# The sort of a graph network's edges: key comparison and rank in six slices among the look-up steps

## The chip, the core and the metric

The kernel runs on one core of a Trainium2 chip. A core has five engines with queues of their own, which work beside one another and meet at semaphores: TensorE (PE, matrix products; its weight loads are listed as PEld), VectorE (DVE), ScalarE (ACT), GpSimd (POOL, here the issuer of indirect DMAs) and SyncE (SP, which issues plain DMAs). The metric is the device time of one execution in microseconds (us), the median of several runs; less is better.

## The reference

Four residual layers of a graph network over 12500 nodes and 412500 edges. Every layer normalises the node features, gathers over the edges and adds the result to `x`:

```python
h = jnp.maximum(_layernorm(x, axis=-1), 0.0)
x = x + _L0_gnn_ref(h, edge_weight1, src, dst, L0_gnn_W, L0_gnn_b)      # weighted sum by dst
h = jnp.maximum(_layernorm(x, axis=-1), 0.0)
x = x + _L1_gnn_ref(h, edge_index, edge_attr_32, L1_gnn_u, batch0, ...) # sum, max, mean of edge_attr by src
h = jnp.maximum(_layernorm(x, axis=-1), 0.0)
x = x + _L2_gnn_ref(h, L2_gnn_weight_r, src, dst, edge_type_8)          # one matrix per edge type
h = jnp.maximum(_layernorm(x, axis=-1), 0.0)
x = x + _L3_gnn_ref(h, L3_gnn_attn_l, L3_gnn_attn_r, src, dst)          # attention over dst
```

The edges come sorted by `dst`, so sums by `dst` are running sums. The second layer sums and maximises by `src`:

```python
seg_sum = jax.ops.segment_sum(edge_attr, row, num_segments=N)   # row = src
seg_max = jax.ops.segment_max(edge_attr, row, num_segments=N)
cnt = jax.ops.segment_sum(jnp.ones((edge_attr.shape[0], 1), ...), row, num_segments=N)
```

For it the kernel first puts the edge features in order of `src`. That sort is what the change touches.

## The kernel before

The padded edges lie on 128 partitions (P) of J columns each. All stages walk over the J columns in NCH = 54 chunks of L = 60 columns; a chunk is 128 x 60 = 7680 edges. Stages follow one another with a barrier between:

- the first third of the weighted sum (`gathered_layer("wsum", ...)`, 18 chunks), in which PE also counts how many edges each source has (matmuls at L706), while POOL gathers rows with 60 indirect DMAs per chunk (L403);
- the sort, `scatter_by_source` (L717 to L940), from about 1850 to 7060 us;
- the other two thirds of the weighted sum, now with the scans over the sorted rows beside it; then the layers with types and with attention.

**What the sort does.** For every edge it works out its place in the array `by_src` and POOL scatters the edge's 33 numbers there. The place is: start of the source's run, plus the edges of this source in earlier columns, plus those in the same column on earlier partitions. The last part is the rank in the column.

Earlier columns: a running count per source lies in the PSUM tile `pC`, laid out as 128 rows (source number modulo 128) by 98 (source number over 128), in WAYS = 4 streams side by side, since columns are taken four at a time. A chunk has STEPS = 15 steps of four columns. For one step, ACT copies the counts (`sort_cnt`, L892, `snapshot`); PE adds the step's edges with four matmuls of one-hots (`low`, `high` into `pC`, L926, `update`) and looks the counts up with matmuls of `lowT` against the copy (into one of three tiles `pG`, L934, `look_up`; each is shown as two in the trace, so eight per step); DVE multiplies by the one-hot `high` (`sort_prod`, L843, `weigh`) and sums it (`sort_place`, L850, `pick`). I count the steps from zero. PE may run three look-ups ahead of `weigh`; the next snapshot waits for the update before it.

The rank in the column: SP loads for each partition the source numbers of all partitions before it (`sort_keys`, 7680 int16 each, 1920 KB) and DVE compares them with the partition's own (L834), then sums over the 128 (L836, into `sort_rank`). The tile is compared in place. The transposed one-hot `lowT` comes from another load, the low seven bits of all edges of the chunk (`sort_lows`, 960 KB, L828).

**Order on DVE**, for every chunk: split the source numbers (L815 to L819), `low` (L824), `high` (L825), `lowT` (L828), comparison (L834), rank (L836), then the 15 steps, each a `weigh` followed by the `pick` of the step before, and at the end `hand_on` (L857), which adds place and rank into `sort_place_i`.

**Order on the others.** SP (L773 to L777) waits until the rank of the chunk before is made, loads keys and low bits under one semaphore, then the features (`sort_feat`, 960 KB). POOL waits for `sort_place_i` and issues 60 scatters (L787), 128 rows each; the places and rows have two buffers, and `hand_on` needs POOL to be a quarter into the batch before. So DVE and PE work on chunk k+1 while POOL scatters chunk k. ACT fills the rows to be scattered from the features in between (L900).

Of the kernel before, what the change touches and what calls it, by code (L numbers as in the profile page):

```python
# [14 lines left out]
P = 128  # L15
# [28 lines left out]
def build(nc, x, src, dst, etype, weight, attr, W0, b0, u, W1, b1, W2, b2, Wr, attn_l, attn_r, out, L):  # L44
# [31 lines left out]
    with ctx:  # L76
# [640 lines left out]
        def scatter_by_source(lead_chunk):  # L717
# [7 lines left out]
            with ExitStack() as c:  # L725
# [3 lines left out]
                def sem(name):  # L729
# [23 lines left out]
                pC = ps("pC", [P, 512], F32, c)  # L753
                loaded = [sem(f"loaded{s}") for s in range(2)]
                scattered = [semaphore(f"scattered{s}") for s in range(2)]
                (rows_ready, rows_used, split, parted, keys_loaded, matched, ranked, ones_ready, based, snapped, updated, summed,
                 picked, placed, place_ready, issuing) = (
                    sem(n) for n in ("rows_ready", "rows_used", "split", "parted", "keys_loaded", "matched", "ranked", "ones_ready",
                                     "based", "snapped", "updated", "summed", "picked", "placed", "place_ready", "issuing"))
                block = phase(c)  # L760
                PIECES = 4
                PIECE = L // PIECES
                earlier_keys = bass.AP(tensor=key_rows.tensor, offset=0, ap=[[L, P], [2 * P * L, NCH], [1, P * L]])
                every_low = bass.AP(tensor=low_rows.tensor, offset=0, ap=[[0, P], [P * L, NCH], [1, P * L]])

                @block.sync
                def _(sp):
                    with sp.Fori(0, NCH // 2) as i:
                        for s in range(2):
                            k = 2 * i + s  # L770

                            sp.wait_ge(ranked, k + 1)
                            sp.dma_start(keys[:].unsqueeze(1), earlier_keys[:, bass.ds(k, 1), :]).then_inc(keys_loaded, 16)  # L773
                            sp.dma_start(lows[:].unsqueeze(1), every_low[:, bass.ds(k, 1), :]).then_inc(keys_loaded, 16)

                            sp.wait_ge(rows_ready, k + 1)
                            sp.dma_start(feat[s][:], attr.rearrange("(p j) f -> p j f", p=P)[:, bass.ds(k * L, L), :]).then_inc(loaded[s], 16)  # L777
# [31 lines left out]
                def _(dve):  # L809
                    v = nc.vector  # L810

                    def one_hots(k):

                        dve.wait_ge(ranked, k + 1)
                        v.tensor_scalar(parts_i[:, 0, :], src_all[:, bass.ds(k * L, L)], 127, None, ALU.bitwise_and)  # L815
                        v.tensor_scalar(parts_i[:, 1, :], src_all[:, bass.ds(k * L, L)], 7, None, ALU.logical_shift_right)
                        v.tensor_copy(parts[:, 2, :], src_all[:, bass.ds(k * L, L)]).then_inc(split, 1)
                        dve.wait_ge(split, k + 1)
                        v.tensor_copy(parts[:, 0:2, :], parts_i[:]).then_inc(parted, 1)  # L819
                        dve.wait_ge(parted, k + 1)  # L820
                        dve.wait_ge(updated, STEPS * k + 1)
                        part = lambda m, w: parts[:, m, :].unsqueeze(2).to_broadcast([P, L, w])
                        iota = lambda w: iota_b[:, 0:w].unsqueeze(1).to_broadcast([P, L, w])
                        v.tensor_tensor(low[:], iota(P), part(0, P), ALU.is_equal)  # L824
                        v.tensor_tensor(high[:], iota(HT), part(1, HT), ALU.is_equal)  # L825

                        dve.wait_ge(keys_loaded, 32 * k + 32)
                        v.tensor_tensor(lowT[:], lows[:].rearrange("p (x j) -> p j x", j=L),  # L828
                                        own_near.unsqueeze(2).to_broadcast([P, L, P]), ALU.is_equal).then_inc(ones_ready, 1)

                    def rank_in_tile(k):

                        by_row = keys[:].rearrange("p (x j) -> p x j", j=L)
                        v.tensor_tensor(by_row, by_row, parts[:, 2, :].unsqueeze(1).to_broadcast([P, P, L]), ALU.is_equal).then_inc(matched, 1)  # L834
                        dve.wait_ge(matched, k + 1)
                        v.tensor_reduce(rank[:], keys[:].rearrange("p (x j) -> p j x", j=L), AX, ALU.add).then_inc(ranked, 1)  # L836

                    def weigh(t, n):

# [22 lines left out]
                        v.tensor_tensor(base[:, w, :], base[:, w - 1, :], streams[:, w - 1, :], ALU.add).then_inc(based, 1)  # L862
                    dve.wait_ge(based, WAYS + 1)
                    v.tensor_copy(own_near, own_part[:]).then_inc(ranked, 1)
                    for n in range(2):
                        dve.sem_inc(placed, 1)
                    for n in range(3):
                        dve.sem_inc(picked, 1)
                    with dve.Fori(0, NCH // 2) as i:
                        for s in range(2):  # L870
                            k = 2 * i + s
                            one_hots(k)
                            rank_in_tile(k)
                            for g in range(STEPS):
                                t, n = k * STEPS + g, s * STEPS + g
                                weigh(t, n)
                                if g >= 1:
                                    pick(t - 1, n - 1, s)
                            pick(k * STEPS + (STEPS - 1), s * STEPS + STEPS - 1, s)
# [33 lines left out]
                def _(pe):  # L913
# [24 lines left out]
                    with pe.Fori(0, NCH // 2) as i:  # L938
                        for s in range(2):
                            k = 2 * i + s  # L940
                            pe.wait_ge(ones_ready, k + 1)
                            for g in range(STEPS):
                                t, n = k * STEPS + g, s * STEPS + g
                                update(t, g)
# [688 lines left out]
```

## Time and profile before

| | us |
|---|---|
| median of 3 runs | 20154.68 |
| lowest and highest | 20152.43, 20169.36 |
| span of the profiled execution | 20183.3 |

| engine | busy us | share of the span |
|---|---|---|
| POOL | 13618.7 | 67% |
| DVE | 8578.8 | 43% |
| ACT | 2766.6 | 14% |
| PE | 2490.0 | 12% |
| PEld | 2157.0 | 11% |

The profiled execution's span is 28.6 us, 0.14%, over the median. The rows further down are from it.

How to read them. A group of the view by lines is one source line on one engine: operation, output and inputs, number of runs; then behind the first bar the busy time in us and the mean of one in ns; behind the second bar the engine's idle time just before these instructions and what ended most of it. A timeline row is start, duration in us, engine, line, operation; the bracket is the idle time of that engine before it and what released it. "Remote" is a release for which the profile names no engine of its own, "issue" a wait for nothing that the profile shows. A matmul's start is recorded, its end is modelled; the time at which another engine goes on is the surer sign of when its result arrived. A row of the stretches gives the engines' busy time in the order named, with the number of instructions behind each.

### The profile page before, as it was taken

What the parts mean: (1) busy time and instruction counts of PE and PEld (TensorE: products, weight loads), DVE (VectorE), ACT (ScalarE), POOL (GpSimd) and SP (SyncE); (2) the same over time, 40 slices, a digit from 0 to 9 for tenths busy, and PEclk for the clock granted to TensorE, in tenths of its full rate; (3) what the DMA queues carried; (4) which work ended last, traced back from release to release, by engine and by line L of the source; (5) the groups of instructions that cost most, each with busy time, mean ns of one, the idle gap of its engine ahead of it and who ended that gap; (6) DMA issues with size and microseconds to landing.
All of it is one profiled execution on the core that took longest, in us unless ns stands there. A gap on an engine that the chain in (4) does not pass through costs nothing. (4 is left out here: it accounts for less than half of the span.)

```text
span 20183.3 us, 69907 instructions
## 1 busy us (share of the span) xinstructions
PE 2490.0 (12%) x17889; PEld 2157.0 (11%) x17889; DVE 8578.8 (43%) x7106; ACT 2766.6 (14%) x1894; POOL 13618.7 (67%) x13469
## 2 busy tenths in 40 slices
PE   1212222222222211111150000000000000000000
PEld 0111222222222200000130000000000000000000
DVE  5666677677677566666621111111113222222223
ACT  0000101101000022222221111111110111111110
POOL 5665566666666666666537777777776777777775
PEclk7555555555555555555575555555555555555555
DMA  3111111111111133333321111111113222222221
GB/s 72 45 41 53 49 50 55 52 50 53 54 50 50 42 106 100 100 100 98 94 71 48 47 47 47 47 47 47 47 46 34 48 48 48 48 48 48 48 48 41
DMA packets 613752, 1142.94 MB, mean 57 GB/s; under 512 B 331103, under 2 KB 383040, under 8 KB 571200
## 3 DMA queue, kind: packets, MB, share of 16 engines
q0 software_dynamic: 430432, 388.76, 10.9%
q10 hardware_dynamic: 34560, 436.30, 5.3%
q1 hardware_dynamic: 148704, 317.25, 5.0%
q8 instruction: 21, 0.34, 0.0%
q14 instruction: 35, 0.29, 0.0%
HBM read 617.82 MB, written 523.59 MB: 57 GB/s over the span
## 5 line engine op out<-in xcount | busy, mean ns | idle before, releaser
L787 POOL DMA_INDIRECT by_src<-H,sort_place_i x3240 | 3146.9, 971 | 1992.3 <-DVE sort_place_i L857 1020.2
L403 POOL DMA_INDIRECT rel_G<-rel_table,rel_idx x3240 | 3475.6, 1073 | 1311.7 <-issue 1031.8
L403 POOL DMA_INDIRECT att_G<-att_table,att_idx x3240 | 3418.0, 1055 | 1095.0 <-issue 1095.0
L403 POOL DMA_INDIRECT lead_rows<-h_table,wsum_idx x3120 | 2956.9, 948 | 1604.2 <-issue 939.1
L562 DVE SCALAR_TENSOR_TENSOR rel_Gf<-rel_Sf,rel_keep_first,rel_Gf 128x64 f32<-128x64 f32 x54 | 18.1, 335 | 4000.4 <-ACT rel_Gf L659 2094.3
L538 DVE TENSOR_TENSOR_SCAN att_near<-att_near,er_in 128x60 f32<-128x60 f32 x54 | 19.1, 354 | 3471.6 <-DMA att_G<-att_table,att_idx 3471.6
L934 PE MATMUL pG<-sort_cnt,sort_lowT 128*128 128x98 f32 x6480 | 1300.8, 366 | 882.7 <-DVE sort_prod L843 500.4
L439 DVE TENSOR_TENSOR wsum_low<-iota_b,wsum_parts 128x3840 fp8e4<-128x3840 bf16 x216 | 896.4, 4150 | 1103.6 <-remote 934.0
L934 PEld LDWEIGHTS pG<-sort_cnt,sort_lowT 128*128 128x128 f32 x6480 | 1181.7, 272 | 891.6 <-DVE sort_prod L843 505.2
L706 PE MATMUL wsum_C<-wsum_high,wsum_low 128*128 128x98 fp8e4 x6480 | 714.4, 266 | 3985.3 <-issue 2780.0
L843 DVE TENSOR_TENSOR sort_prod<-pG,sort_high 128x392 f32<-128x392 f32 x810 | 453.5, 565 | 1529.1 <-remote 1169.9
L892 ACT COPY sort_cnt<-pC 128x392 f32<-128x392 f32 x810 | 393.7, 486 | 4634.6 <-PE pC L926 2548.0
L706 PEld LDWEIGHTS wsum_C<-wsum_high,wsum_low 128*128 128x128 fp8e4 x6480 | 523.4, 130 | 4176.4 <-issue 4176.1
L659 ACT COPY rel_Gf<-rel_G 128x3840 f32<-128x3840 f32 x54 | 359.6, 6659 | 3280.7 <-DMA rel_G<-rel_table,rel_idx 3280.7
L836 DVE TENSOR_REDUCE sort_rank<-sort_keys 128x60 f32<-128x7680 int16 x54 | 785.7, 14550 | 1.9
L926 PE MATMUL pC<-sort_high,sort_low 128*128 128x98 bf16 x3240 | 363.7, 251 | 2841.0 <-DVE sort_lowT L828 1649.5
L828 DVE TENSOR_TENSOR sort_lowT<-sort_lows,sort_side 128x7680 f32<-128x7680 uint8 x54 | 707.5, 13101 | 0.0
L440 DVE TENSOR_TENSOR wsum_high<-iota_b,wsum_parts 128x2940 fp8e4<-128x2940 bf16 x216 | 693.2, 3209 | 0.0
L645 ACT COPY pool_S<-H 128x2880 f32<-128x2880 f32 x72 | 368.2, 5114 | 2089.8 <-DVE H L467 1465.4
L926 PEld LDWEIGHTS pC<-sort_high,sort_low 128*128 128x128 bf16 x3240 | 305.9, 131 | 2885.5 <-issue 2048.9
L665 ACT COPY wsum_S<-wsum_Sf 128x3840 f32<-128x3840 f32 x54 | 363.0, 6723 | 1658.0 <-DVE wsum_Sf L568 1558.1
L1079 PE MATMUL pR<-ident,att_tail 128*66 128x128 f32 x2 | 0.7, 436 | 4628.4 <-DVE att_fk L1014 4628.4
(389 smaller groups left out, 7825.7 us busy)
## 6 DMA issues: line engine op xcount, KB each, us to landing
scan_att<-att_S ACTq DMA_DIRECT2D x54, 1980.0 KB
scan_wsum<-wsum_S ACTq DMA_DIRECT2D x54, 1920.0 KB
sort_keys<-key_rows SPq DMA_DIRECT2D x54, 1920.0 KB
scan_pool<-pool_S ACTq DMA_DIRECT2D x72, 1440.0 KB
scan_rel<-rel_S ACTq DMA_DIRECT2D x54, 1920.0 KB
pool_row<-by_src SPq DMA_DIRECT2D x36, 1485.0 KB
sort_lows<-low_rows SPq DMA_DIRECT2D x54, 960.0 KB
sort_feat<-in_attr SPq DMA_DIRECT2D x54, 960.0 KB
```

The source lines that it names most:

```text
L403: pool.indirect_dma_start(out=G[s][:, j, :], out_offset=None, in_=table, in_offset=bass.IndirectOffsetOnAxis(ap=idx[s][:, j:j + 1], axis=0 ...
L439: v.tensor_tensor(low[b][:], iota(P), part(0, P), ALU.is_equal, saturate=False)
L440: v.tensor_tensor(high[b][:], iota(HT), part(1, HT), ALU.is_equal, saturate=False).then_inc(oh_ready, 1)
L645: nc.scalar.copy(pS[:].rearrange("p j f -> p f j"), pSf[:, :, rows]).then_inc(ptaken, 1)
L706: last = mm(C[:, w * HT:(w + 1) * HT], low[g % NB][:, j, :], high[g % NB][:, j, :], start=False, stop=False, skip_group_check=True)
L787: pool.indirect_dma_start(out=by_src, out_offset=bass.IndirectOffsetOnAxis(ap=place_i[s][:, j:j + 1], axis=0), in_=row[s][:, j, :], in_off ...
L828: v.tensor_tensor(lowT[:], lows[:].rearrange("p (x j) -> p j x", j=L), own_near.unsqueeze(2).to_broadcast([P, L, P]), ALU.is_equal).then_i ...
L836: v.tensor_reduce(rank[:], keys[:].rearrange("p (x j) -> p j x", j=L), AX, ALU.add).then_inc(ranked, 1)
L843: v.tensor_tensor(prod[n % 2][:], pG[n % 3][:, 0:W].rearrange("p (w h) -> p w h", w=WAYS), high[:, WAYS * g:WAYS * (g + 1), :], ALU.mult). ...
L892: a.copy(cnt[n % 2][:], pC[:, 0:W]).then_inc(snapped, 1)
L926: last = mm(pC[:, w * HT:(w + 1) * HT], low[:, WAYS * g + w, :], high[:, WAYS * g + w, :], start=False, stop=False, skip_group_check=True)
L934: last = mm(pG[n % 3][:, w * HT:(w + 1) * HT], lowT[:, WAYS * g + w, :], cnt[n % 2][:, w * HT:(w + 1) * HT], start=True, stop=True, skip_g ...
```

## The change

The comparison and the rank sum of a chunk, one instruction of 128 x 7680 each, become six each of 128 x 1280: ten of the 60 columns at a time, for all 128 earlier partitions. Slice e is compared just before the `weigh` of step 2e and summed just behind it, so e = 0 to 5 stand at the steps 0, 2, 4, 6, 8 and 10. The semaphore `ranked` is raised by the last sum. Keys and low bits get a semaphore each. SP asks for the low bits of the next chunk when `lowT` is written (`ones_ready`, which gets one more count at the start), and for the keys when the last rank sum is done; the features follow behind the keys as before. PE's wait counts one further for the same reason.

```diff
+                            sp.wait_ge(ones_ready, k + 1)
+                            sp.sem_inc(loading, 1)
+                            sp.dma_start(lows[:].unsqueeze(1), every_low[:, bass.ds(k, 1), :]).then_inc(lows_loaded, 16)
                             sp.wait_ge(ranked, k + 1)
+                            sp.sem_inc(loading, 1)
                             sp.dma_start(keys[:].unsqueeze(1), earlier_keys[:, bass.ds(k, 1), :]).then_inc(keys_loaded, 16)
-                            sp.dma_start(lows[:].unsqueeze(1), every_low[:, bass.ds(k, 1), :]).then_inc(keys_loaded, 16)
...
-                    def rank_in_tile(k):
-
-                        by_row = keys[:].rearrange("p (x j) -> p x j", j=L)
-                        v.tensor_tensor(by_row, by_row, parts[:, 2, :].unsqueeze(1).to_broadcast([P, P, L]), ALU.is_equal).then_inc(matched, 1)
-                        dve.wait_ge(matched, k + 1)
-                        v.tensor_reduce(rank[:], keys[:].rearrange("p (x j) -> p j x", j=L), AX, ALU.add).then_inc(ranked, 1)
+                    def match_slice(k, e):
+
+                        if e == 0:
+                            dve.wait_ge(keys_loaded, 16 * k + 16)
+                        cols = slice(e * SLICE, (e + 1) * SLICE)
+                        by_row = keys[:].rearrange("p (x j) -> p x j", j=L)[:, :, cols]
+                        v.tensor_tensor(by_row, by_row, parts[:, 2, cols].unsqueeze(1).to_broadcast([P, P, SLICE]),
+                                        ALU.is_equal).then_inc(matched, 1)
+
+                    def rank_slice(k, e):
+
+                        dve.wait_ge(matched, SLICES * k + e + 1)
+                        cols = slice(e * SLICE, (e + 1) * SLICE)
+                        last = v.tensor_reduce(rank[:, cols], keys[:].rearrange("p (x j) -> p j x", j=L)[:, cols, :], AX, ALU.add)
+                        if e == SLICES - 1:
+                            last.then_inc(ranked, 1)
...
-                            rank_in_tile(k)
                             for g in range(STEPS):
                                 t, n = k * STEPS + g, s * STEPS + g
+                                if g % 2 == 0 and g // 2 < SLICES:
+                                    match_slice(k, g // 2)
                                 weigh(t, n)
+                                if g % 2 == 0 and g // 2 < SLICES:
+                                    rank_slice(k, g // 2)
                                 if g >= 1:
                                     pick(t - 1, n - 1, s)
...
-                            pe.wait_ge(ones_ready, k + 1)
+                            pe.wait_ge(ones_ready, k + 2)
```

What stands in a row on DVE at the start of a chunk's steps, before (`sort_side` is the PSUM tile that holds the source numbers and their parts; `pG0` to `pG2` are the three look-up tiles):

```order
L828 TENSOR_TENSOR sort_lowT<-sort_lows,sort_side 128x7680 [waits sort_keys_loaded]
L834 TENSOR_TENSOR sort_keys<-sort_keys,sort_side 128x7680
L836 TENSOR_REDUCE sort_rank<-sort_keys 128x60 [waits sort_matched]
L840 REGISTER_ALU
L843 TENSOR_TENSOR sort_prod0<-pG0,sort_high 128x392 [waits sort_placed,sort_summed]
L840 REGISTER_ALU
L841 REGISTER_ALU [waits sort_summed]
L843 TENSOR_TENSOR sort_prod1<-pG1,sort_high 128x392 [waits sort_placed]
L850 TENSOR_REDUCE sort_place0<-sort_prod0 128x4 [waits sort_picked]
```

And now, at the same place on DVE:

```order
L833 TENSOR_TENSOR sort_lowT<-sort_lows,sort_side 128x7680 [waits sort_lows_loaded]
L842 TENSOR_TENSOR sort_keys<-sort_keys,sort_side 128x128x10 [waits sort_keys_loaded]
L855 REGISTER_ALU
L858 TENSOR_TENSOR sort_prod0<-pG0,sort_high 128x392 [waits sort_placed,sort_summed]
L847 ISA
L849 TENSOR_REDUCE sort_rank<-sort_keys 128x10 [waits sort_matched]
L855 REGISTER_ALU
L856 REGISTER_ALU [waits sort_summed]
L858 TENSOR_TENSOR sort_prod1<-pG1,sort_high 128x392 [waits sort_placed]
L865 TENSOR_REDUCE sort_place0<-sort_prod0 128x4 [waits sort_picked]
L842 TENSOR_TENSOR sort_keys<-sort_keys,sort_side 128x128x10
```

The first `weigh` stands behind one slice of the comparison and not behind the whole of it and the rank; from there on every second step carries a slice of both.

SP's loop over a chunk, before:

```order
L773 ISA [waits sort_ranked]
L773 DMA sort_keys<-key_rows 128x7680
L774 REGISTER_ALU
L774 DMA sort_lows<-low_rows 128x7680
L777 ISA [waits sort_rows_ready]
L777 DMA sort_feat<-in_attr 128x1920
```

And now:

```order
L776 REGISTER_ALU [waits sort_ones_ready]
L776 DMA sort_lows<-low_rows 128x7680
L779 ISA [waits sort_ranked]
L779 DMA sort_keys<-key_rows 128x7680
L782 ISA [waits sort_rows_ready]
L782 DMA sort_feat<-in_attr 128x1920
```

The load of the low bits has moved ahead of the keys and has a wait of its own.

## Rows read from the trace of the kernel before

**Rows 1.** Groups by line, costliest first; columns as explained in the section on the profile.
```profile
L787 POOL DMA_INDIRECT by_src<-H,sort_place_i x3240 | 3146.9, 971 | 1992.3 <-DVE sort_place_i L857 1020.2 <-issue 972.1
...
L836 DVE TENSOR_REDUCE sort_rank<-sort_keys 128x60 f32<-128x7680 int16 x54 | 785.7, 14550 | 1.9
...
L843 DVE TENSOR_TENSOR sort_prod<-pG,sort_high 128x392 f32<-128x392 f32 x810 | 453.5, 565 | 1529.1 <-remote 1169.9 <-PE pG L934 283.1 <-issue 35.9
...
L850 DVE TENSOR_REDUCE sort_place<-sort_prod 128x4 f32<-128x392 f32 x810 | 441.5, 551 | 0.0
...
L834 DVE TENSOR_TENSOR sort_keys<-sort_keys,sort_side 128x7680 int16<-128x7680 int16 x54 | 439.2, 8133 | 0.0
```

**Rows 2.** One tile, `sort_place_i`: count, ns min/median/max, first and last start.
```profile
L857 DVE TENSOR_TENSOR sort_place_i<-sort_place,sort_rank x54: 221/222/223, 1949.9 to 6986.1; 128x60 int32<-128x60 f32 x54
```

**Rows 3.** Busy time by stretch, two chunks of the sort (columns PE, PEld, DVE, ACT, POOL).
```profile
4423.90:4515.70 91.80, 27.32 (x180) 26.25 (x180) 65.94 (x39) 9.40 (x20) 58.33 (x61) 0.57 0.17 54
4515.70:4611.80 96.10, 24.68 (x180) 23.82 (x180) 66.45 (x42) 9.40 (x20) 58.23 (x61) 0.57 0.16 52
```

**Rows 4.** Timeline of the sort, chunk A.
```profile
4451.39 0.51 PE L926 MATMUL pC<-sort_high,sort_low 128*128 128x98 bf16 x4 [30.41 <-DVE sort_lowT L828]
...
4474.43 2.03 PE L934 MATMUL pG<-sort_cnt,sort_lowT 128*128 128x98 f32 x8 [16.62 <-DVE sort_prod L843]
...
4487.82 0.57 DVE L843 TENSOR_TENSOR sort_prod<-pG,sort_high 128x392 f32<-128x392 f32 x1 [6.03 <-remote]
...
4499.22 0.97 POOL L787 DMA_INDIRECT by_src<-H,sort_place_i  x1 [0.30 <-issue]
...
4500.46 0.57 DVE L843 TENSOR_TENSOR sort_prod<-pG,sort_high 128x392 f32<-128x392 f32 x1 [11.61 <-remote]
...
4503.38 0.57 DVE L843 TENSOR_TENSOR sort_prod<-pG,sort_high 128x392 f32<-128x392 f32 x1 [1.88 <-remote]
...
4514.62 0.22 DVE L857 TENSOR_TENSOR sort_place_i<-sort_place,sort_rank 128x60 int32<-128x60 f32 x1 [0.19 <-DVE sort_place L850]
...
4515.66 0.97 POOL L787 DMA_INDIRECT by_src<-H,sort_place_i  x1 [15.46 <-DVE sort_place_i L857]
```

**Rows 5.** Timeline of the sort, chunk B, the one behind it.
```profile
4568.48 0.53 PE L926 MATMUL pC<-sort_high,sort_low 128*128 128x98 bf16 x4
...
4574.05 0.49 ACT L892 COPY sort_cnt<-pC 128x392 f32<-128x392 f32 x1 [22.74 <-remote]
...
4592.93 0.57 DVE L843 TENSOR_TENSOR sort_prod<-pG,sort_high 128x392 f32<-128x392 f32 x1 [23.11 <-remote]
...
4596.55 0.57 DVE L843 TENSOR_TENSOR sort_prod<-pG,sort_high 128x392 f32<-128x392 f32 x1 [2.59 <-remote]
...
4610.76 0.22 DVE L857 TENSOR_TENSOR sort_place_i<-sort_place,sort_rank 128x60 int32<-128x60 f32 x1 [0.19 <-DVE sort_place L850]
...
4611.80 0.97 POOL L787 DMA_INDIRECT by_src<-H,sort_place_i  x1 [19.87 <-DVE sort_place_i L857]
```

**Rows 6.** The key loads (first and last issue), and the sort's last chunk.
```profile
L773 SPq DMA_DIRECT2D sort_keys<-key_rows x54: 332/333/381, 1850.1 to 6845.3; - x54
...
6965.15 0.57 DVE L843 TENSOR_TENSOR sort_prod<-pG,sort_high 128x392 f32<-128x392 f32 x1 [20.18 <-remote]
...
6971.45 0.49 ACT L892 COPY sort_cnt<-pC 128x392 f32<-128x392 f32 x1 [21.43 <-remote]
```

**Rows 7.** Timeline of the stage ahead of the sort, one batch of POOL.
```profile
524.20 0.95 POOL L403 DMA_INDIRECT lead_rows<-h_table,wsum_idx  x1 [15.95 <-PE wsum_C L706]
...
534.33 2.61 PE L706 MATMUL wsum_C<-wsum_high,wsum_low 128*128 128x98 fp8e4 x30 [10.92 <-issue]
...
541.52 2.53 PE L706 MATMUL wsum_C<-wsum_high,wsum_low 128*128 128x98 fp8e4 x29 [4.58 <-DVE wsum_high L440]
...
556.08 0.24 PE L706 MATMUL wsum_C<-wsum_high,wsum_low 128*128 128x98 fp8e4 x1 [2.55 <-issue]
```

**Rows 8.** Busy time of one stretch of chunk A; the last columns are clock, DMA, GB/s.
```profile
4475.00:4487.70 12.70, 9.04 (x55) 8.59 (x54) 4.46 (x9) 1.95 (x4) 9.68 (x10) 0.63 0.95 323
```

More of the change, by code:

```diff
@@ L755, in scatter_by_source @@
                 scattered = [semaphore(f"scattered{s}") for s in range(2)]
-                (rows_ready, rows_used, split, parted, keys_loaded, matched, ranked, ones_ready, based, snapped, updated, summed,
+                (rows_ready, rows_used, split, parted, keys_loaded, lows_loaded, loading, matched, ranked, ones_ready, based, snapped, updated, summed,
                  picked, placed, place_ready, issuing) = (
-                    sem(n) for n in ("rows_ready", "rows_used", "split", "parted", "keys_loaded", "matched", "ranked", "ones_ready",
+                    sem(n) for n in ("rows_ready", "rows_used", "split", "parted", "keys_loaded", "lows_loaded", "loading", "matched", "ranked", "ones_ready",
                                      "based", "snapped", "updated", "summed", "picked", "placed", "place_ready", "issuing"))
@@ L762, in scatter_by_source @@
                 PIECE = L // PIECES
+                SLICES = 6
+                SLICE = L // SLICES
                 earlier_keys = bass.AP(tensor=key_rows.tensor, offset=0, ap=[[L, P], [2 * P * L, NCH], [1, P * L]])
@@ L825, in one_hots @@
                         v.tensor_tensor(high[:], iota(HT), part(1, HT), ALU.is_equal)
-                        dve.wait_ge(keys_loaded, 32 * k + 32)
+                        dve.wait_ge(lows_loaded, 16 * k + 16)
                         v.tensor_tensor(lowT[:], lows[:].rearrange("p (x j) -> p j x", j=L),
                                         own_near.unsqueeze(2).to_broadcast([P, L, P]), ALU.is_equal).then_inc(ones_ready, 1)
-                    def rank_in_tile(k):
-                        by_row = keys[:].rearrange("p (x j) -> p x j", j=L)
-                        v.tensor_tensor(by_row, by_row, parts[:, 2, :].unsqueeze(1).to_broadcast([P, P, L]), ALU.is_equal).then_inc(matched, 1)
-                        dve.wait_ge(matched, k + 1)
-                        v.tensor_reduce(rank[:], keys[:].rearrange("p (x j) -> p j x", j=L), AX, ALU.add).then_inc(ranked, 1)
+                    def match_slice(k, e):
[11 more added lines that the diff above has]
+                            last.then_inc(ranked, 1)
                     def weigh(t, n):
@@ L864, in _ @@
                     v.tensor_copy(own_near, own_part[:]).then_inc(ranked, 1)
+                    dve.sem_inc(ones_ready, 1)
                     for n in range(2):
```

## The prediction

> **What bounds the kernel now.** I read the groups by line first. The change touches only the sort stage, so the question is what that stage waits for. Its 3240 scatters keep POOL busy, and before each of the 54 batches POOL waits for the places (`sort_place_i`): 1020.2 us in all, 18.9 us per batch [rows 1]. The first and last `sort_place_i` stand 5036.2 us apart, 53 periods of 95.0 us [rows 2]. POOL issues for 76.6 us of each (60 scatters of 0.971 us with 0.30 us between, 972.1 us over 3186 gaps [rows 1]) and stands idle for the rest. A microsecond cut from the idle time ahead of a batch is cut from the kernel, until nothing of the 18.9 us is left.
>
> Who makes POOL wait? Not DVE's amount of work: the windows over two neighbouring chunks show it busy for 65.9 of 91.8 us and 66.5 of 96.1 us, and PE for about 27 and 25 us [rows 3]. I call the chunks A (4423.9 to 4515.7) and B (4515.7 to 4611.8). The timelines show the waits. In A, `lowT` is ready at 4451.4, PE starts its look-ups, runs three ahead and is stopped for 16.6 us, because DVE sits in the whole-tile comparison (8.1 us) and the rank sum (14.6 us) [rows 1, 4]. When DVE comes back the steps run smoothly for a while; then, with PE's matmuls all started long before, DVE gets the results late: gaps of 6.0 and 11.6 us, put down to "remote" [rows 4]. In B one gap is 23.1 us [rows 5]. Over the stage these gaps are 1169.9 us [rows 1], 21.7 us per chunk, almost all of DVE's idle time. ACT sees the same: in B the four `pC` matmuls start at 4568.48 and take 0.53 us, but the copy that waits for them starts at 4574.05 [rows 5].
>
> **When do the late results end?** In A POOL's last scatter starts at 4499.22; the results arrive at 4500.46 and 4503.38. In B POOL's batch ends about 4591.9 (19.87 us before 4611.80), and they arrive at 4592.93 and 4596.55. In the last chunk it is the same (6965.15, 6971.45), although the last of the 54 key loads was issued at 6845.3, so it isn't the loads [rows 4 to 6]. In the stage before, where PE has the same POOL beside it, 30 matmuls take 2.61 us, 29 more 2.53 us, and later in the same batch single ones stand 2.6 us apart; this slowness begins about 21 us into POOL's batch, after some 60 matmuls with their weight loads [rows 7], while in the sort it begins 57 us (A) and 53 us (B) into the batch. So I read it like this: beside POOL's indirect DMAs PE's results pass freely up to a certain number and then slowly, and the rest of the chunk's 15 steps must wait until POOL's batch has ended. What POOL waits for is this tail.
>
> **The change part by part.** (1) The comparison and the sum leave the place ahead of the steps. PE isn't stopped for 16.6 us [rows 4] any more. (2) They come back as six pairs, each placed around the steps 0, 2, ... 10, counted from zero. A compare of 392 elements takes 565 ns and one of 7680 takes 8133 ns [rows 1]: 1.04 ns an element and 0.16 us fixed. Six slices of 1280 cost 6 x 1.49 = 8.9 us, 0.8 more than now. The sum is 14.55 us; a sum of 392 elements takes 0.55 us [rows 1], so its fixed part is at most that. I take 0.14 us, near the compare's: six of 2.56 us, 0.8 us more. (At 0.55 us each the addition would be 2.8 us.) Below nothing it can't go, for the elements and their stride stay. A pair is 4.05 us, all DVE work rises by 1.6 us to some 68 us per chunk, still under POOL's 76.6. (3) The low bits are asked for as soon as `lowT` is made, the keys and features after the last sum. All three transfers together keep the DMA busy for some 12 us [rows 8]. The keys now leave after step 10 and are first read after four more steps and the next chunk's one-hots, some 30 us later, so this costs nothing; without that cover it would cost up to 12 us a chunk. SP waits at `ones_ready` with the keys' load queued behind it, but the keys can't go before the last sum anyway, and the features behind them are read only at step 2 of the next chunk. PE's wait for `ones_ready` is the same wait with its count raised by one.
>
> **What the tail becomes.** Here is the whole balance. At POOL's end DVE has weighed 7 steps in A and 4 in B (the gaps of 6.0 and 23.1 us stand before the 7th and the 5th of them). In A 8 steps are left. From 4500.46 to the places at 4514.62 it is 14.2 us [rows 4]; 8 steps of 0.565 + 0.551 and a last sum are 9.5, so 4.7 us of it is idle and could hide a slice. In the new order the pairs of steps 8 and 10 are still undone: 8.1 - 4.7 = +3.4 us. In B 11 steps are left: from 4592.93 to 4610.76 it is 17.8 us [rows 5], 12.8 busy, 5.0 idle; undone are the sum of step 4 and three pairs, 14.7 - 5.0 = +9.7 us. The mean is **+6.5 us** per chunk if as many steps are done at POOL's end as now.
> Against that, PE gets the 16.6 us in which it stood still. Had these been at the pace of the late stretch (in A two steps from 4487.82 to 4503.38, 0.13 a us; in B one in the 23.1 us, 0.04 a us), 0.7 to 2.1 more steps are over when POOL ends. Each takes 1.12 us and half a pair, 2.0 us, out of the tail: 2.2 to 6.6 us, the middle of which I take, **-4.4 us**, since A's and B's patterns both fill the stage. Sum: +2.1 us x 53 = +111 us. Against the profile's own span of 20183.3 us this gives 20294; the median of the runs is 20154.7, 28.6 us (0.14%) lower, and the prediction is made at it: **20265 us**. Its own range, from the two ends, is -5 to +228 us: 20150 to 20383.
>
> **The rivals.** *Nothing gained ahead of POOL's end* (slower): the number of steps that pass beside POOL is fixed by the count of PE's instructions; then starting them earlier only makes the late stretch begin earlier, and the slices stand in the tail in full. +6.5 us x 53 = +345 us, 20500. For it speaks the stage before, where slowness began after 60 matmuls at 21 us. It decides if DVE still has weighed only 4 to 7 steps at POOL's end.
> *The late stretch begins by the clock* (faster): in A and B it begins 57 and 53 us into the batch. DVE starts 28 us into it and needs 3.15 us a step (two steps and a pair in 6.3), so 8.6 steps are over by then, and one to three more by the end: 4.5 are left, all slices are done. The tails of A and B (8 and 11 left, 15.5 and 19.9 us [rows 4, 5]) differ by 1.47 us a step; 4.5 left make 10.3 us, 8.6 less than 18.9: -456 us, 19700. Rows 7 speak against it.
> *The late stretch goes away* (much faster): PE's results were late for a reason that the new order removes, and DVE's 68 us fit under POOL's 76.6. The wait of 18.4 us goes in each period: -975 us, 19180. Here a rule can be weighed. By the rows above, PE's results come late as long as POOL issues [rows 4 to 6]. The Trainium skill, SBUF — State Buffer, section "Who interferes with whom", says that PE and ACT never wait on anyone. By that rule the delay isn't POOL's doing at the memory's ports, and this rival would be open; the measured rows decide for me, since the delay ends with the batch in all three places.
> *Nothing moves*: PE's results are limited per period, whatever the order; earlier steps and longer tail cancel. 20155.
>
> **How the numbers follow.** Chances: the forecast 0.42, nothing gained 0.20, by the clock 0.22, gone 0.05, nothing moves 0.11. About 0.2% (40 us) is what a measurement can tell from no change. Of the forecast's 0.42 its lower end gives 0.08 to the same and 0.02 to faster. Faster: 0.22 + 0.05 + 0.02 = 0.29. Same: 0.11 + 0.08 = 0.19. Slower: 0.52. The range takes in the fall to 19700 with 50 us of play, and the rise to 20500 with 50 more for the sum's larger fixed part: 19650 to 20550.
>
> **What would show it.** In the new trace: (a) twelve slices of 1.49 and 2.56 us; (b) no stop of 16.6 us in PE's look-ups; (c) DVE's "remote" gaps still there, beginning earlier in POOL's batch and ending with it; (d) steps weighed at POOL's end: 5 to 9, with sums and compares behind it; (e) POOL's wait for `sort_place_i` at 21 us instead of 18.9. Ten or more steps weighed, and a wait near 10 us, would make the third case right; gaps gone, the fourth; a wait of 25 us, the second. The other stages should keep their times.

## The result, and the profile after

The changed kernel takes 20672 us (median of 4 runs, 20667 to 20692), the kernel before 20162 us (median of 4) beside it: a ratio of 1.025, 95% interval 1.0237 to 1.0263. The change costs 510 us. The prediction was 20265 us with a range of 19650 to 20550: the sign was right, the size was not, and the time lies outside the range.

These are the page's groups of the changed kernel that answer to [rows 1], from an execution with a span of 20690.1 us (line, engine, operation, tiles and count, busy us and mean ns, idle time of the engine ahead of them and what ended it):

```profile
L792 POOL DMA_INDIRECT by_src<-H,sort_place_i x3240 | 3137.2, 968 | 2509.9 <-DVE sort_place_i L872 1538.9
...
L403 POOL DMA_INDIRECT rel_G<-rel_table,rel_idx x3240 | 3473.4, 1072 | 1314.4 <-issue 1034.0
...
L953 PE MATMUL pG<-sort_cnt,sort_lowT 128*128 128x98 f32 x6480 | 1350.3, 376 | 238.6 <-DVE sort_prod L858 238.3
L439 DVE TENSOR_TENSOR wsum_low<-iota_b,wsum_parts 128x3840 fp8e4<-128x3840 bf16 x216 | 896.4, 4150 | 1106.1 <-remote 1004.4
...
L849 DVE TENSOR_REDUCE sort_rank<-sort_keys 128x10 f32<-128x1280 int16 x324 | 829.3, 2559 | 0.0
```

POOL's wait for the places grew from 1020.2 us [rows 1] to 1538.9: from 18.9 to 28.5 us per batch, +9.6. That is the whole loss: 519 us more of waiting, 10 us less for the scatters themselves (3146.9 and 3137.2 us), and a span that grew by 507. POOL itself works as before, and the look-ups on PE stand half as long behind DVE (238.3 us against 500.4): the change does what it says, and it makes POOL wait longer.

One chunk of the sort shows how. These are rows of DVE, PE and POOL (start us, us, engine, line, operation, tiles, and in brackets the idle time ahead of it):

```profile
4500.73 0.57 DVE L858 TENSOR_TENSOR sort_prod<-pG,sort_high 128x392 f32<-128x392 f32 x1 [1.08 <-PE pG L953]
...
4513.92 1.99 PE L953 MATMUL pG<-sort_cnt,sort_lowT 128*128 128x98 f32 x8
...
4522.90 0.57 DVE L858 TENSOR_TENSOR sort_prod<-pG,sort_high 128x392 f32<-128x392 f32 x1 [10.23 <-remote]
...
4546.01 0.96 POOL L792 DMA_INDIRECT by_src<-H,sort_place_i  x1 [0.30 <-issue]
4549.53 0.57 DVE L858 TENSOR_TENSOR sort_prod<-pG,sort_high 128x392 f32<-128x392 f32 x1 [23.14 <-remote]
...
4552.95 2.58 DVE L849 TENSOR_REDUCE sort_rank<-sort_keys 128x10 f32<-128x1280 int16 x1
...
4564.90 2.56 DVE L849 TENSOR_REDUCE sort_rank<-sort_keys 128x10 f32<-128x1280 int16 x1
...
4573.14 0.22 DVE L872 TENSOR_TENSOR sort_place_i<-sort_place,sort_rank 128x60 int32<-128x60 f32 x1 [0.19 <-DVE sort_place L865]
```

POOL's batch runs from 4470.9 to 4547.0. The steps begin 30 us into it (in the kernel before 50 us), five of them are weighed, and PE's results come late as before: DVE waits 10.23 and 23.14 us, and gets the sixth result 2.5 us after POOL's end. PE had started this step's look-ups at 4513.92, 35.6 us before DVE could use them. Ten steps are left (9.6 in the mean in the kernel before), but now three of the six slice pairs stand among them. The places follow at 4573.1, POOL's next batch at 4574.2.

Counted over all batches, 5 steps are weighed when POOL's batch ends in 52 of the 53 chunks (6 in one). In the kernel before it was 4 in 25 chunks, 5 in 6, 6 in 4, 7 in 12 and 8 in 6, a mean of 5.4. Its POOL stood idle for 20.9, 19.6, 17.4, 16.1 and 15.0 us in these groups, 18.74 in the mean; in the changed kernel it is 28.2. (A step counts as weighed when its `weigh` has started.) So the same number of steps done (5 and 5) costs 19.6 and 28.2 us, **+8.6 us** by the slices; the first figure rests on six chunks only. The other 0.9 is the difference in the mix of chunks.

### The profile page after: what moved, and what is told of

Same layout as the page of the kernel before. It is cut to its first block and busy times, and to the rows that moved or that the text cites. A ratio compares the mean times of both kernels' runs of the same rounds, so it can differ in the third digit from the quotient of the medians.

```text
span 20690.1 us, 70882 instructions
## 1 busy us (share of the span) xinstructions
PE 2590.8 (13%) x17889; PEld 2208.5 (11%) x17889; DVE 8598.6 (42%) x7646; ACT 2766.1 (13%) x1894; POOL 13598.0 (66%) x13469
## 5 line engine op out<-in xcount | busy, mean ns | idle before, releaser
L792 POOL DMA_INDIRECT by_src<-H,sort_place_i x3240 | 3137.2, 968 | 2509.9 <-DVE sort_place_i L872 1538.9
L403 POOL DMA_INDIRECT rel_G<-rel_table,rel_idx x3240 | 3473.4, 1072 | 1314.4 <-issue 1034.0
L953 PE MATMUL pG<-sort_cnt,sort_lowT 128*128 128x98 f32 x6480 | 1350.3, 376 | 238.6 <-DVE sort_prod L858 238.3
L439 DVE TENSOR_TENSOR wsum_low<-iota_b,wsum_parts 128x3840 fp8e4<-128x3840 bf16 x216 | 896.4, 4150 | 1106.1 <-remote 1004.4
L849 DVE TENSOR_REDUCE sort_rank<-sort_keys 128x10 f32<-128x1280 int16 x324 | 829.3, 2559 | 0.0
```

The source lines that it names most:

```text
L403: pool.indirect_dma_start(out=G[s][:, j, :], out_offset=None, in_=table, in_offset=bass.IndirectOffsetOnAxis(ap=idx[s][:, j:j + 1], axis=0 ...
L439: v.tensor_tensor(low[b][:], iota(P), part(0, P), ALU.is_equal, saturate=False)
L792: pool.indirect_dma_start(out=by_src, out_offset=bass.IndirectOffsetOnAxis(ap=place_i[s][:, j:j + 1], axis=0), in_=row[s][:, j, :], in_off ...
L849: last = v.tensor_reduce(rank[:, cols], keys[:].rearrange("p (x j) -> p j x", j=L)[:, cols, :], AX, ALU.add)
L953: last = mm(pG[n % 3][:, w * HT:(w + 1) * HT], lowT[:, WAYS * g + w, :], cnt[n % 2][:, w * HT:(w + 1) * HT], start=True, stop=True, skip_g ...
```

## The experiments

**What a reader must know of the occasions.** Kernels that were measured together ran on one chip, beside the kernel before. At the first measurement and on one of six later occasions the kernel before took 20162 and 20295 us, with PE's late results. On the other five it took 17295 to 17327 us, and none were late. Each of the six was another chip, so the runs don't say whether it is the chip or a condition of it. I call them *late* and *free* occasions and compare inside an occasion alone. On the late one the trace speaks to the prediction directly. On the free one it doesn't, unless the late results are imitated. All ratios are against the kernel before of the same occasion, with the 95% interval.

**The parts alone, and where the slices stand** (a free occasion). e1_slices_only keeps the two loads together (the low bits' line moves here from ahead of the wait):

```
 sp.wait_ge(ranked, k + 1)
 sp.sem_inc(loading, 1)
 sp.dma_start(keys[:].unsqueeze(1), earlier_keys[:, bass.ds(k, 1), :]).then_inc(keys_loaded, 16)
+sp.dma_start(lows[:].unsqueeze(1), every_low[:, bass.ds(k, 1), :]).then_inc(lows_loaded, 16)
```

e2_loads_only keeps the rank whole and ahead of the steps (`SLICES = 1`, `match_slice(k, 0)` and `rank_slice(k, 0)` behind `one_hots(k)`). e3_early has `SLICES = 5` and `if g < SLICES`. e5_mid has the whole rank behind the `weigh` of step 3.

> The six slices as in the changed kernel, but the low bits are loaded with the keys after the last sum, as before. Theory S (the three pairs behind the end of POOL's batch are the cost): 20640 to 20700 us, POOL's wait for the places 28 us per batch, 5 steps weighed when POOL's batch ends. Rival L (the low bits' load, now 30 us earlier beside POOL's scatters, makes PE's results late): near 20160 us, wait 19 us.

> The other part alone: the low bits are loaded as soon as lowT is made, the comparison and the sum stay whole and ahead of the steps. Theory S: 20130 to 20200 us, wait 19 us, as before. Rival L: 20500 us or more.

> The changed kernel with five slices of 12 columns at the steps 0, 1, 2, 3 and 4 in place of six at 0, 2 ... 10, so that all stand ahead of the end of POOL's batch. Theory S: the number of steps weighed at that end stays at 5 and no pair is left, so the wait of 28.2 us falls by the 9.4 us that the changed kernel has more: 18 to 20 us, the time 20100 to 20220 us. Rival D (cutting the rank into pieces between the steps costs by itself, through the handshakes between DVE, PE and ACT, wherever the pieces stand): 20600 to 20700 us.

> The whole comparison and the whole sum (23 us) in one piece between the weighing of step 3 and that of step 4. Theory S: they lie in the stretch in which DVE would wait for PE's late results; 4 or 5 steps are weighed at POOL's end and 10 or 11 are left, as in the kernel before: wait 17 to 20 us, 20050 to 20220 us. Rival T (the late results depend on the clock since the batch began, and only the steps' early start in the changed kernel is of worth): the stop of 23 us costs steps, wait 24 us or more, 20430 us or more.

Measured: 17300.0 (1.0001, 0.9992 to 1.0011), 17297.9 (1.0002), 17297.6 (1.0000) and 17302.2 us (1.0002, 0.9993 to 1.0012) against 17295.4. Nothing tells them apart, since the thing to be told apart wasn't there. e4_late (slices at the steps 4, 6 ... 14) and e8_lookups_twice (each look-up matmul issued twice) met the same on a second free occasion:

> The changed kernel with its six slices at the steps 4, 6 ... 14 in place of 0, 2 ... 10. Where PE's results come late (a chip on which the kernel before needs 20160 us): theory S (a pair behind the end of POOL's batch costs 3.1 us, a third of the changed kernel's 9.4): all six pairs are behind it, wait 28.2 + 9.4 = 37.6 us, 21170 us; rival D (cutting costs by itself, wherever the pieces stand): 20670 us. Where they don't (a chip on which the kernel before needs 17295 us): DVE's 68 us stay under POOL's 76.4, no wait, 17300 us.

> The changed kernel with each look-up matmul issued twice into the same place: 12 matmuls a step in place of 8, the same signals. On a chip with late results: theory C (the limit is a count of PE's instructions): 3 or 4 steps are weighed at POOL's end in place of 5, one or two more pairs are left, wait 31 us or more, 20850 us or more. Rival H (the limit is a count of PE's signals to the other engines, two a step): 5 steps, 20670 to 20750 us. On a chip without them: 17300 us, as PE has room.

Measured 17297.6 (0.9999, 0.9989 to 1.0008) and 17296.0 (1.0001, 0.9991 to 1.0010) against 17295.7. Even six slices late in the chunk cost nothing there, nor do 20 matmuls a step, as the trace counts them, in place of 12. So two rivals stay without a test of their own on a late occasion: that loading the low bits early makes PE's results late, and that cutting the rank costs by itself. Whether the late results are counted in PE's instructions or in its signals stays open.

**The changed kernel on the free occasion**, unchanged:

> The changed kernel as it is, on this second chip, on which the kernel before needs 17295 us. DVE's 68 us a chunk stay under POOL's 76.4, so every chunk's places are ready before POOL asks for them: 17290 to 17310 us, all 15 steps weighed when POOL's batch ends. Rival: with the slices the chain DVE, PE, ACT is longer than 76.4 us per chunk: over 17350 us.

Measured 17299.7 us against 17297.5: 1.0000 (0.9991 to 1.0010). The page's groups, from a span of 17293.9 us:

```profile
L403 POOL DMA_INDIRECT rel_G<-rel_table,rel_idx x3240 | 3066.9, 947 | 1087.2 <-issue 987.1
L792 POOL DMA_INDIRECT by_src<-H,sort_place_i x3240 | 3138.0, 969 | 987.4 <-issue 987.4
...
L439 DVE TENSOR_TENSOR wsum_low<-iota_b,wsum_parts 128x3840 fp8e4<-128x3840 bf16 x216 | 895.9, 4148 | 13.1 <-DVE wsum_parts L431 13.1
...
L858 DVE TENSOR_TENSOR sort_prod<-pG,sort_high 128x392 f32<-128x392 f32 x810 | 456.0, 563 | 464.3 <-PE pG L953 424.4
```

POOL never waits for places: its idle time is the 0.30 us between scatters. The weighings wait 464.3 us in all, 424.4 of them put down to PE itself and none to "remote", where the kernel before on the late occasion had 1529.1 [rows 1]. The scatters last as long as before (969 ns); it is PE's results that come in time. With the places ready long ahead, POOL is the bound of the sort, 76.4 us a chunk against DVE's 68, and the order of DVE's work costs nothing, whichever it is.

**The late results imitated** (a third free occasion). One wait holds PE ahead of a chunk's step 5 until POOL is at its batch's end, in the kernel before, in the changed one and in e3_early's order:

```
 # POOL, behind the 60 scatters of a batch, and once ahead of the first
+pool.sem_inc(batch_over, 1)
 # PE
+if g == 5:
+    pe.wait_ge(batch_over, k + 1)
 update(t, g)
```

> The kernel before with one wait added: PE makes its first five steps of a chunk freely and step 5 only when POOL has issued the last scatter of its batch, as the late results of the first chip had it in all chunks of the changed kernel. Theory S: the tail is then the same as there: the chunks of the kernel before with 5 steps weighed had 19.6 us of POOL idle, of which 4.4 us were until the first late result, here some 1.6: wait 16 to 19 us, 18130 to 18290 us.

> The same wait in the changed kernel. Theory S: three pairs stand behind it and cost 8.6 us a chunk more than in the kernel before with the wait, as between the two kernels' chunks of 5 steps on the first chip: wait 25 to 28 us, 455 us (430 to 480) more than g5_before. Rival H (beside late results the slices are hidden in gaps between the steps, and what cost time on the first chip was something that the late results did to the slices): less than 200 us more than g5_before.

> The same wait with five slices at the steps 0 to 4, none behind the wait. Theory S: as g5_before, within 1 us a chunk: within 53 us of it. Rival D (cutting costs by itself): as g5_after.

Measured 17374.7 us (1.0043, 1.0026 to 1.0060), 17880.7 (1.0339, 1.0321 to 1.0356) and 17382.1 (1.0047, 1.0030 to 1.0064). POOL's queue runs ahead of POOL by some 15 us: PE takes up step 5 at 61 us of the batch and not at 76, and the absolute times are lower than expected by this. The difference stands, for POOL still waits for the places in every batch: **the changed kernel is 506 us slower than the kernel before** (theory S had 455, at most 480; the late occasion had 510), and with all slices ahead of the stop it is 7 us. That kernel too is cut and loads the low bits early, so here neither costs anything beyond these 7 us, which lie within the 30 us or so by which each ratio is uncertain (rival D falls here). What the early load does to late results no run shows. The wait for the places in g5_before and g5_after (time and times):

```profile
  DVE sort_place_i L859: 89.9, 52
```

```profile
  DVE sort_place_i L874: 584.2, 52
```

That is 494 us more. g5_late (another free occasion; six slices at the steps 4 to 14, so that five pairs stand behind the stop) gave a third point:

> The six slices at the steps 4, 6 ... 14, with the wait of g5_before (PE's step 5 only when POOL's sequencer has issued the last scatter). Five pairs stand behind the wait. Theory S, by the 9.5 us that the three pairs of g5_after cost over g5_before (3.16 us each): 15.8 us a chunk over g5_before, 840 us more: 18215 us on a chip without late results. Rival H (what is hidden of a pair is a fixed 2.7 us a chunk, so that each further pair costs its full 4.05 us): 9.5 + 8.1 = 17.6 us, 18305 us. On a chip with late results: wait 35 us or more, over 21000 us.

Measured 18297.4 us (1.0558, 1.0540 to 1.0575) against 17327.3, 970 us more, with 962.8 us of waiting for the places; g5_before had 77 more than its own kernel before. That leaves 893 us or 16.8 us a chunk, between theory S's 15.8 and rival H's 17.6. The period of POOL's batches is 77.85, 87.32 and 94.79 us with none, three and five pairs behind the stop: 9.5 us for the first three and 7.5 for two more, 3.7 each. So each further pair is paid in full, and only the first ones hide a little. How much can be read off: between its first result behind the stop and the places, DVE waits 1.55 us a chunk in g5_before and not at all in g5_after, and 3 x 3.67 - 1.55 is the 9.5. H was right in kind, with a pair at 3.7 us in line and not 4.05.

**The same on a late occasion** (the kernel before at 20295 us). The signal comes here from a memset of one column behind POOL's last scatter, so that it is given when POOL has executed it; the wait stands ahead of step 4, or of step 7.

> The kernel before with one wait: PE makes steps 0 to 3 of a chunk freely and step 4 only when POOL has executed the last scatter of its batch (a memset of one column behind it signals). On the first chip the chunks of the kernel before with 4 steps weighed at POOL's end had 1.6 us until the next weighing, 18.35 us from there to the places and 1.0 us to the next batch: wait 20.9 us, 18390 us (18340 to 18440).

> The same wait in the changed kernel: what the prediction worked out for its chunk B, +9.7 us a chunk over the kernel before with as many steps weighed (14.7 us of slices behind the stop, 5.0 of them hidden): 514 us more than h4_before. Theory S, by the price a pair has shown (9.5 us for three, 0.78 of its duration): 14.7 x 0.78 = +11.5 us, 610 us more.

> The kernel before with the same wait ahead of step 7. By the chunks of 7 steps on the first chip (13.2 us from the first late weighing to the places): wait 15.7 us, 18110 us (18060 to 18160).

> The changed kernel with the wait ahead of step 7. The prediction's working for chunk A: two pairs behind the stop, 8.1 us of which 4.7 are hidden: +3.4 us a chunk, 180 us more than h7_before. Theory S by the price that a pair has shown: 2 x 3.16 = +6.3 us, 335 us more.

Measured 20295.0 us (1.0004, 0.9994 to 1.0013), 20966.2 (1.0329, 1.0312 to 1.0346), 20292.1 (0.9999) and 20785.7 (1.0244, 1.0227 to 1.0261); I had reckoned with a free occasion, hence the absolute numbers. With 4 steps weighed in every chunk, the kernel before loses nothing, and the changed one is 671 us behind it: **+12.7 us a chunk where the prediction had +9.7** and theory S 11.5. The wait ahead of step 7 was hardly ever reached: PE's results were late before it, and h7_after has 5 steps weighed in all 53 chunks, h7_before 4 in 37, 5 in 9 and 7 in 7. So these two are the kernel before and the changed one once more, 494 us apart, and chunk A's +3.4 could not be tested. POOL's wait for the places is 1092.6 us in h4_before and 1782.1 us in h4_after.

And the tail on DVE. h4_before, from the first late result to the places:

```profile
4445.87 0.57 DVE L846 TENSOR_TENSOR sort_prod<-pG,sort_high 128x392 f32<-128x392 f32 x1 [25.55 <-PE pG L937]
...
4447.01 0.57 DVE L846 TENSOR_TENSOR sort_prod<-pG,sort_high 128x392 f32<-128x392 f32 x1
...
4459.01 0.22 DVE L860 TENSOR_TENSOR sort_place_i<-sort_place,sort_rank 128x60 int32<-128x60 f32 x1 [0.19 <-DVE sort_place L853]
```

h4_after, the same stretch:

```profile
4572.69 0.57 DVE L861 TENSOR_TENSOR sort_prod<-pG,sort_high 128x392 f32<-128x392 f32 x1 [35.56 <-PE pG L956]
...
4576.31 0.57 DVE L861 TENSOR_TENSOR sort_prod<-pG,sort_high 128x392 f32<-128x392 f32 x1
...
4577.26 1.48 DVE L845 TENSOR_TENSOR sort_keys<-sort_keys,sort_side 128x1280 int16<-128x1280 int16 x1
...
4582.26 0.57 DVE L861 TENSOR_TENSOR sort_prod<-pG,sort_high 128x392 f32<-128x392 f32 x1
...
4599.26 0.22 DVE L875 TENSOR_TENSOR sort_place_i<-sort_place,sort_rank 128x60 int32<-128x60 f32 x1 [0.19 <-DVE sort_place L868]
```

Read the gaps between weighings. Without slices and without waiting they are 1.14 us (4445.87, 4447.01), which is the weighing and the sum back to back. Two steps with a pair take 5.95 us (4576.31 to 4582.26), 3.67 more. The first of these chunks is one of the shortest of h4_before, 13.1 us; over all 53 it is 14.7 us, and 1.6 of them are waits of DVE between the first weighings. In h4_after it is 26.6 us in the mean and there are no such waits. So the three pairs and a sum (13.5 us) cover 1.6 us of waiting, and the first late result comes 0.8 us later (5.3 us behind POOL's end and not 4.5): 12.7.

**Does a short silence of POOL let further steps pass?** Two kernels make POOL wait inside its batch for a step of DVE's: p2_before_pause at scatter 45, p1_after_pauses at four places.

```
 for j in range(L):
+    if j in PAUSES and not (isinstance(k, int) and k == NCH - 1):
+        pool.wait_ge(picked, STEPS * k + (STEPS + 4 + PAUSES[j]))
+        pool.sem_inc(issuing, 1)
```

> Five slices at the steps 0 to 4, asked for again in the hope of a chip on which PE's results come late (the kernel before at 20150 to 20300 us there). Theory S: 4 or 5 steps are weighed at POOL's end with at most one pair behind it, wait 19 to 22 us in place of the changed kernel's 28: within 1% of the kernel before. Rival D (cutting costs by itself): 2.5% more. On a chip without late results: 17300 us.

> The kernel before with one wait added in POOL's batch: ahead of its scatter 45 (57 us into the batch) POOL waits until DVE has weighed step 5 of the chunk. On a chip with late results: theory R (POOL's silence lets PE's results through, and the free count starts again): POOL stands still for 2 to 6 us, then at least four more steps pass freely; 9 or more are weighed at its end, POOL's idle time there falls from 20.2 to 13 us or less, pauses and idle together to 15 to 18 us: 100 to 280 us less than the kernel before. Rival N (nothing starts again; only the end of the whole batch frees the results): the pause is added, 5 to 6 steps weighed at the end, 100 to 250 us more. On a chip without late results the steps are weighed long before: 17300 us.

> The changed kernel with four waits in POOL's batch: ahead of the scatters 36, 42, 48 and 54 POOL waits until DVE has weighed the steps 4, 6, 8 and 10 of the chunk. On a chip with late results: theory R (POOL's silence lets PE's results through and the free count starts again): each stop lasts 2 to 5 us and 11 or more steps are weighed at the batch's end, where 8 us or less of idle are left: 20100 to 20500 us against the changed kernel's 20672. Rival N (silence frees only what waits, the count doesn't start again): each stop frees one or two steps, the four stops cost 12 to 20 us and the wait at the end falls by less: 20700 us or more. On a chip without late results: 17300 us.

All three met free occasions: e3b_early 17303.0 us (1.0002, 0.9992 to 1.0011), p2_before_pause 17298.6 (0.9999, 0.9989 to 1.0008), p1_after_pauses 17329.2 against 17327.3 (1.0001, 0.9992 to 1.0011). They show that these waits cost nothing where the step they wait for was weighed long before. What they do where results are late is open, and so is whether one of them beats the kernel before there.

## Why the sign was right and the size wrong

**What bounds the kernel.** Right: POOL's wait for `sort_place_i` took all of the loss, and this wait is the tail behind POOL's end. It holds on the late occasion alone. On the free one the case that the prediction called *the late stretch goes away* is what both kernels do: a period of 76.4 us where it had 76.6. The sign came from this wait, and from slices that stand in it.

**The slices' price (part 2).** The durations came as said, 1.48 and 2.56 us. In line with steps a pair takes 3.67 us of DVE and not 4.05, since it fills small gaps between weighing and sum.

**The loads (part 3).** That they cost nothing fits g5_early, which has them and is 7 us over g5_before. On a late occasion the early load was never seen without the slices.

**The balance.** These are the terms of the prediction's sum, in us a batch, beside the means of the 53 batches in the traces of the two kernels. A step without waiting is put at 1.14 us and a pair at 3.67 us, as read above.

| term | predicted | measured |
|---|---|---|
| pairs behind POOL's end | +11.4 | +11.0 (3.0 pairs) |
| DVE's waits behind the first late result, which slices can fill | -4.85 | -3.75 (3.95, now 0.20) |
| more steps ahead of POOL's end | -4.4 | +0.4 (5.4 steps, now 5.0) |
| time from POOL's end to the first late result | not in it | +1.8 (2.25, now 4.04) |
| sum | +2.1 | +9.5 |

**The -4.4 us for more steps ahead of POOL's end.** This is the step that failed, in sign and size; it is 4.8 of the 7.4 us that are missing. I had PE's free 16.6 us buy 0.7 to 2.1 steps at the late stretch's pace. The steps did start 20 us earlier in the batch, and the late stretch simply began earlier: 39 to 45 us into the batch in place of 54 to 59 (start of DVE's first wait of over 3 us). At POOL's end stood 5.0 steps where it had been 5.4. That is the rival *nothing gained ahead of POOL's end*: it asked for 4 to 7 steps and a wait of 25 us, and got 5 and 28.5. The stage ahead [rows 7] spoke for it, and I named it, but gave it 0.20 and let the pace of two gaps carry the forecast.

**The +6.5 us of the tail.** This one was right in kind and too small. It let 4.7 to 5.0 us of each tail hide slices, and slices do fill DVE's waits there: 0.20 us of them are left. But there is less to fill than A and B together promise. Behind the first late result the kernel before waits 5.25 us in its chunks with 4 steps weighed and 3.5 with 7, but only 2.2 with 5 steps, 3.95 in the mean of all; and in the changed kernel 52 of 53 chunks are chunks with 5. Held against those, three pairs of 3.67 us less 2.0 hidden, and a first late result 0.4 us earlier, are the +8.6 of above. Against all chunks, the first late result comes 1.8 us later, which the sum had put at nothing; why it does is not shown. The g5 pair has +9.5, with 1.55 us to hide. The h4 pair's +12.7 doesn't test the 5.0 us of B: the stop moves most of that wait ahead of the first result, where no slice stands (1.6 us are left of the 5.25 of such chunks, and POOL's idle time is nearly the same, 20.2 and 20.9 us).

What these waits are, B shows:

```profile
4599.34 0.57 DVE L843 TENSOR_TENSOR sort_prod<-pG,sort_high 128x392 f32<-128x392 f32 x1 [1.75 <-PE pG L934]
```

```profile
4597.00:4601.00 4.00, 4.00 (x27) 3.99 (x28) 1.62 (x4) 1.47 (x3) 0.00 (x0) 0.56 0.00 0
4601.00:4609.00 8.00, 7.86 (x85) 7.69 (x82) 7.24 (x14) 3.90 (x8) 0.00 (x0) 1.00 0.00 0
```

One is another late result (2.59 us [rows 5]). The next two, 1.75 and 0.72 us, are PE itself: it had stood still for 20 us, and its granted clock (third number from the end) is 0.56 at first, mostly the lower of the two levels (1.2 GHz), and then 1.00 (2.4 GHz). At the lower level a step's eight look-up matmuls take 1.99 us, at the higher one 1.09, and DVE needs 1.14 us a step.

The sort's first batch starts 17.8 us later on top (1968.8 against 1951.0).

**The range.** Its upper end was *nothing gained* with 6.5 us, plus 50. With the 9.5 us measured it would have been 20708, and 20672 would lie inside. So the range failed by that case's size, not by a case left out.

**Slips in the working.** POOL's batch is 76.3 us (60 scatters and 59 gaps), not 76.6. With 0.14 us fixed a sum of 1280 comes to 2.54 us and not 2.56; measured are 2.56. The slow matmuls of the stage ahead start 1.4 to 2.8 us apart, and 2.6 is only the longest idle time before one. In the last chunk the result at 6965.15 comes 2.4 us ahead of the batch's end. None of these carries the result.

**The other rivals.** *The late stretch begins by the clock* falls: between the kernels it moved by 12 us with the steps' start. *Nothing moves* falls: the tail grew and nothing made up for it. *Gone* falls on the late occasion. There DVE waits up to 25.7 us for PE's results beside POOL (kernel before), while the matmuls had been started in time. The rule of the Trainium skill, SBUF — State Buffer, section "Who interferes with whom", that PE and ACT never wait on anyone, doesn't cover this; the page speaks of the memory's ports, and the rows here don't say that these are where the delay arises.

**What would show it.** (a) held. (b) held: PE's look-ups stand 238.3 us behind DVE where it was 500.4, and no stop of 16 us. (c) held: the gaps begin earlier and end with the batch. (d) gave 5, the lowest of "5 to 9". (e) gave 28.5 us where 21 was named, past the 25 of the rival.

**Still open:** why PE's results come late on some occasions and not on others, and in what unit the free number is counted. Five steps are 60 matmuls, about as many as ran freely in the stage ahead [rows 7], but the kernel before has 4 steps, 48 matmuls, in 25 of its chunks. No run separates these.

## What to carry to other kernels

Where an engine sits out a wait that has a fixed end, work belongs ahead of the waiting instruction: behind it, it is added to the tail (three pairs of 3.67 us cost 8.6 to 9.5), because the queue is in order and the tail is that engine's own. Starting a stalled chain earlier gains nothing if the stall is set by what the chain has already done; look whether the stall moves with the start. And before an idle stretch is counted as cover, look on which side of the moved instruction it lies, and whether the new order still has chunks of the kind in which it was read.

## What the runs showed of the hardware

The same program ran in 20162 and 20295 us on two occasions and in 17295 to 17327 us on five, each stable within 0.3%. Beside POOL's indirect DMAs DVE waits up to 25.7 us for results of PE that the profile puts down to "remote" on the first kind (25.2 us in the changed kernel), and never on the second, with the same scatters of 0.97 us. The gathers from `rel_table` differ as well: 1072 ns on the late occasion and 947 ns on the free one. The stage ahead of the sort shows it too: DVE's `wsum_low` waited 1106.1 us in the changed kernel there, and 13.1 us in the same kernel here. A 2.5% loss on one occasion was 0.0% on the other, so a change in the order of work beside POOL has to be timed on both.
